# Mixing steps of DVE moved ahead of and behind the one-hots, with new shares of the one-hots and new slots for the tiles on PE

## What is computed

```python
xn = layernorm(x)
shifted = pad(xn)[:, :-1]                       # the token before
xk = xn * mix_k + shifted * (1 - mix_k)         # likewise xv and xr
k, v, r = xk @ Wk.T, xv @ Wv.T, sigmoid(xr @ Wr.T)
s = (r * wkv_scan(decay, first, k, v)) @ Wo.T
probs = softmax(xn @ w_router.T)
top_w, top_e = top_k(probs, 4); top_w /= sum(top_w)
for e in range(16):
    coeff = sum(where(top_e == e, top_w, 0))
    ffn += coeff * ((silu(xn @ w_gate[e]) * (xn @ w_up[e])) @ w_down[e])
out = x + s * silu(ffn)
```

## Time and profile before

| | us |
|---|---|
| median of 3 runs | 324.53 (323.92 to 325.04) |
| the profiled execution | 324.29 |
| its span in the trace | 322.5 |
| outside the span | 1.79 |
| PE busy | 287.6 (89% of the span) |
| DVE busy | 251.2 (78%) |
| POOL busy | 203.7 (63%) |
| ACT busy | 146.0 (45%) |

### The profile page before, as it was taken

One profiled execution on the slowest core, in us unless ns is written; L12 is line 12 of the kernel. 1 busy time (PEld: TensorE's weight loads), 2 busy tenths in 40 slices (PEclk: granted clock), 3 DMA queues, 4 the chain that ended last, 5 costly groups with the idle time before them and its releaser, 6 DMA issues.

```text
span 322.5 us, 4601 instructions
## 1 busy us (share of the span) xinstructions
PE 287.6 (89%) x1298; PEld 212.3 (66%) x1299; DVE 251.2 (78%) x523; ACT 146.0 (45%) x219; POOL 203.7 (63%) x201
## 2 busy tenths in 40 slices
PE   0698969979889999999999999999999999969960
PEld 0443424434335665888888888888888888848850
DVE  2889799986986888689299896898869961439993
ACT  1791726423267752841935536465273232312140
POOL 3600089993773767778778787787777776242281
PEclk9999979999999999999999999999999999988995
DMA  7896000016377676459655454655556578899798
GB/s 230 285 374 287 0 1 1 0 34 244 99 236 273 226 272 218 146 212 291 217 199 170 149 213 148 227 160 192 171 168 207 155 221 301 265 337 303 223 230 163
DMA packets 30379, 63.28 MB, mean 196 GB/s; under 512 B 4332, under 2 KB 20205, under 8 KB 30192
## 3 DMA queue, kind: packets, MB, share of 16 engines
q10 hardware_dynamic: 7568, 23.88, 21.2%
q0 software_dynamic: 8544, 19.41, 21.2%
q1 hardware_dynamic: 14240, 19.66, 18.1%
HBM read 50.35 MB, written 15.20 MB: 203 GB/s over the span
## 4 chain that ended last, share of the span: by engine, by line
PE 60%; DVE 16%; DMA 12%; issue 4%; ACT 3%; POOL 3%; ACTq 1%; SPq 0%; DVEq 0%; POOLq 0%
PE ps L589 52%; DMA rows<-wgu_in 5%; PE ps L696 4%; DVE arena L848 3%; DVE ohB L1007 2%; DMA y_rows<-arena,dst_idx 2%; PE ps L599 2%; DVE ohA L1002 2%; DMA wrou<-wrouT_in 1%; DMA rows<-y_rows 1%; DVE arena L1136 1%; DMA y_rows<-arena,late 1%; POOL arena L393 1%; POOL y_rows L400 1%; DVE arena L1103 1%
## 5 line engine op out<-in xcount | busy, mean ns | idle before, releaser
L589 PE MATMUL ps<-arena,rows 128*128 128x256 f32 x448 | 102.8, 384 | 3.1 <-DMA rows<-wgu_in 3.1
L393 POOL DMA_INDIRECT arena<-xn_rows,tok_idx x72 | 79.6, 1106 | 26.2 <-issue 21.6
L589 PEld LDWEIGHTS ps<-arena,rows 128*128 128x128 f32 x448 | 84.1, 193 | 13.9 <-issue 3.5
L400 POOL DMA_INDIRECT y_rows<-arena,dst_idx x60 | 65.2, 1086 | 26.2 <-issue 16.5
L589 PE MATMUL ps<-wdn,arena 128*128 x288 | 67.8, 380 | 0.4 <-DVE arena L1036 0.4
L589 PEld LDWEIGHTS ps<-wdn,arena 128*128 128x128 f32 x288 | 54.2, 191 | 7.7 <-issue 0.8
L589 PE MATMUL ps<-arena 128*128 128x512 f32 x96 | 47.1, 624 | 3.1 <-DVE arena L848 3.1
L549 ACT COPY arena<-ps 128x512 f32<-128x512 f32 x34 | 19.9, 586 | 63.9 <-PE ps L589 55.0
L375 POOL TENSOR_SCALAR ohB<-late 128x128 f16<-128x128 f32 x20 | 31.4, 1581 | 26.3 <-DVE late L924 26.3
L1036 DVE TENSOR_TENSOR arena<-arena,ps 128x512 f32<-128x512 f32 x28 | 19.1, 683 | 33.5 <-PE ps L589 15.3
L539 ACT ACTIVATE arena<-ps 128x512 f32<-128x512 f32 x36 | 21.5, 598 | 35.0 <-PE ps L589 34.9
(11 more groups left out here) (185 smaller groups left out, 370.9 us busy)
## 6 DMA issues: line engine op xcount, KB each, us to landing
rows<-wgu_in ACTq DMA_DIRECT2D x44, 512.0 KB, 3.9
rows<-y_rows SPq DMA_DIRECT2D x6, 768.0 KB, 7.2
wdn<-wd_in SPq DMA_DIRECT2D x1, 4096.0 KB, 14.9
rT<-x_in SPq DMA_DIRECT2D x4, 512.0 KB, 6.4
xn_rows<-rT SPq DMA_DIRECT2D x4, 512.0 KB, 3.3
rows<-y_rows SPq DMA_DIRECT2D x8, 256.0 KB, 4.9
out<-x_in SPq DMA_DIRECT2D x1, 1536.0 KB, 9.5
rows<-y_rows SPq DMA_DIRECT2D x3, 512.0 KB, 5.7
```

Of the source, the lines that this page charges most:

```text
L393: pool.indirect_dma_start(out=xg[i % XG][:, j, :], out_offset=None, in_=xn_rows, in_offset=bass.IndirectOffsetOnAxis(ap=tok_idx[:, 2 * i + ...
L400: pool.indirect_dma_start(out=y_rows, in_=ysb[:, par, j, :], in_offset=None, out_offset=bass.IndirectOffsetOnAxis(ap=idx[:, n + j:n + j + ...
L589: ins = nc.tensor.matmul(dst, lhsT(c), rhs(c), start=(c == 0), stop=(c == C - 1))
```

## The change

The first mixing step of the loop, (1, 0), now stands ahead of DVE's wait for the counts. The others inside the loop move up, (3, 0) stays before the one-hots of tile 11, and (3, 1) now stands behind all one-hots and ahead of DVE's wait for the last tile. DVE makes three ohB of every tile and POOL one, so 48 and 16 instead of 44 and 20. On PE a first tile is placed already after the first product of `project(1)`, and the last tiles after the first product of `project(3)`.

```diff
-        dve_slots = lambda t: 3 if t % 4 else 2
+        dve_slots = lambda t: TOPK - 1
...
             project(0, between0)
-            project(1, lambda n: place_rows((0, 1, 1, 1, 1, 2)[n]))
+            project(1, lambda n: place_rows((1, 1, 1, 1, 1, 1)[n]))
             count_ended()
-            project(2, lambda n: place_rows((1, 1, 1, 2, 1, 1)[n]))
-            project(3, lambda n: place_rows((2, 1, 0, 0, 0, 0)[n]))
+            project(2, lambda n: place_rows((1, 1, 1, 2, 1, 2)[n]))
+            project(3, lambda n: place_rows((2, 0, 0, 0, 0, 0)[n]))
...
+            mixed(1, 0)
             dve.wait_ge(count_ready, 1)
...
-            MIX_AT = {0: (1, 0), 2: (1, 1), 4: (1, 2), 6: (2, 0), 8: (2, 1), 9: (2, 2), 11: (3, 0), 13: (3, 1)}
+            MIX_AT = {0: (1, 1), 2: (1, 2), 4: (2, 0), 6: (2, 1), 8: (2, 2), 11: (3, 0)}
...
+            mixed(3, 1)
             dve.wait_ge(oh_used, T)
```

## The result

The changed kernel took 322.14 us (median of 4 runs, 320.91 to 323.57), the kernel before 324.78 on the same chip (323.92 to 328.34). The ratio is 0.9899, with a 95% interval from 0.9858 to 0.994: faster, by between 0.6% and 1.4%. The profiled execution took 323.57, with a span of 321.8; that is 0.7 less than the 324.29 and 322.5 of before, and the upper end of the four. A second measurement of the unchanged file, on another chip, gave 319.42 (6 runs, 319.16 to 323.59) against 326.4, ratio 0.9835 [0.9774 to 0.9897].

A forecast was written before the change was run, and what follows sets the result against it. PE was taken as the bound, its third-stage start mattering: projections to 78.8, indices 72.4 plus gather lag 6.31 and 0.4, so 79.1 instead of 83.03. That 3.9 us gain gave 320.4, or 320.6 as median; range 319.4 to 322.3.

The forecast's parts named there:

- The counts and the start of the loop: DVE before the one-hots: mixing step (1, 0) makes the counts 0.35 to 0.4 us later, one-hots starting at 41.98.
- The idle time of PE: PE ahead of tile 0: idles 3.25 us until 45.0, replacing the old wait, with product 6 already done.
- DVE's loop: DVE's one-hot loop: shrinks from about 29.9 to 27.6 us, ending at 69.6.
- The near tie: Last two tiles, second stage: PE gets there at 69.0 us, DVE's last one-hot comes at 69.6.
- PE has only 0.6 us in hand: PE after tile 0's wait: 0.6 us of slack; a half-clock stretch would lose 1.67 and make PE late by 1.1.
- the likeliest case: Whole kernel: gain 3.9 us as summed, half clock off the path, time 320.6 us; chance 0.55.
- The second rival: PE's second stage: half clock on the path in most executions, gain only 3.0 us, time 321.5; chance 0.22.
- (3, 1) and the indices: DVE behind the one-hots: (3, 1) runs 69.6 to 70.95, delaying the indices about 1 us, to 72.4.
- The gather: Indices to third stage: lag 6.31 us plus 0.4 for sharing DMA with weight loads; without the 0.4, 78.7 beside PE's 78.8.
- a meeting without any rub: Start of third stage: PE, DVE and POOL meet smoothly and the gather is free, giving 78.4 and 4.6 us gain.
- The fourth rival: Third stage near 286 us: the last-weights wait grows by the gain, its load meeting reads of y; 324.3 to 324.6; chance 0.05.
- The fifth rival: One-hot loop: POOL stands still under DVE's one-hots too, adding 12.7 us to the loop, about 332.8 us; chance 0.05.

The follow-up runs named there:

- after_again: The changed kernel without an edit, measured again on another chip: median 319.42 us of 6 runs, ratio 0.9835 to the kernel before.
- fill_fit: Changed kernel plus thrown-away PE matmuls in two waits, 14 ahead of tile 0 and 7 ahead of the last batch's routing: 321.56 us, ratio 0.9874.
- undo_slots: Changed kernel with the tiles placed on PE in their old slots: median 319.37 us of 4 runs, ratio 0.9896 to the kernel before.
- undo_slots2: Changed kernel with the tiles in their old slots on PE, measured a second time: median 321.29 us of 6 runs, ratio 0.9878.
- after: The changed kernel as first measured and profiled: median 322.14 us of 4 runs, ratio 0.9899; the profiled execution took 323.57.
- probe: Changed kernel with scratch work added ahead of the one-hot loop, 18 POOL one-hots beside four kinds of DVE instruction: 347.31 us, no comparison.
- undo_shares: Changed kernel with the old one-hot shares, 44 on DVE and 20 on POOL: median 322.8 us of 10 runs, ratio 0.9939.
- best: Changed kernel with the x-to-out copy later, mixing steps moved behind tile 0, two POOL one-hots at tiles 7 and 12: 323.24 us, ratio 0.9849.

## Why the prediction was right, and where not

**The counts and the start of the loop.** Predicted 0.35 to 0.4 later, at 41.98. In after_again they came 0.43 and 0.44 later (35.18, 42.04): right. In the first profile the loop began at 44.29, from a slow product at 15 us and a half-clock stretch at 31.2, neither of them in the sum.

**The idle time of PE.** Predicted 3.25 us, a wait of the same length in place of the old one, with one product more behind it; measured 3.17, and 3.49 in after_again. Right.

**DVE's loop.** Predicted 27.6; 27.63 in two profiles. The number was right for partly wrong reasons: the loop holds waits for PE of 0.50 us (0.23 + 0.27), and without the half clock it takes 27.15 (fill_fit).

**PE's placing, and the tie.** Predicted 24.0 us from tile 0 to the last two; 24.10 in fill_fit, with PE there 27.35 us behind the loop's start and DVE ready at 27.15. The near tie was real.

**"PE has only 0.6 us in hand".** This is the step that failed. I took DVE as the later of the two by 0.6 us, and let the likeliest case leave the half clock off the path. All five profiles with the new slots, the mixing table of the change or nearly so, and no filling have the stretch behind the idle time, PE had nothing in hand, and the whole 1.68 us reached the first L696 (fill_fit). The second rival, which I gave 0.22, is what the stage did: it put the first L696 at 80.0, and after_again has it at 80.05. What neither case saw is that the gathers stand behind it as the next limit: without the half clock PE starts sooner, waits 1.15 to 1.54 us for rows, and is level again (undo_slots, undo_slots2). That the stretch cost nothing in the kernel before is not shown either: behind it DVE waited 0.59 us for PE, before 50.50, the idle time that the sum takes out of the loop.

The Trainium skill says in TensorE: Matmul & The Clock Gate (Part 1: The HAM clock gate) that the moment at which the clock changes varies from run to run. The trace agrees for the counts, where a stretch from about 31 us on came in two of fourteen profiles (after, and at 31.4 the probe, ahead of its added work); at tile 0, behind 3.1 to 3.5 us of idling, it came every time, in five profiles.

**POOL.** Predicted 25.6 us behind the loop's start and the waits at tiles 10 and 12 gone. It was 27.05, 1.4 later (it waits for buffers that PE frees, six times 0.26 to 0.50), and the two waits are gone. The shares were not needed for that: undo_shares has no such waits either.

**(3, 1) and the indices.** Predicted 30.4 behind the loop's start, measured 31.03. That (3, 1) would delay the indices by 1 us did not happen: DVE was done with it 0.60 us before the tile was, since the tile came with PE.

**The gather.** The lag was to be 6.31 + 0.4 and a tie with PE. From the end of the indices (75.32) to the first L696 it was 6.98 here, but PE took the rows without waiting, directly behind the last product, so this is no longer the gather's lag. In undo_slots, where PE waited 0.28 for them, it was 36.54 - 30.82 = 5.72: the extra 0.4 was not there, nor even the whole 6.31. What I missed is the unit behind: I costed the first gather alone, while the following ones hang on the same indices.

**The end.** Predicted 79.1 for the start of the third stage, 3.9 us gained. Measured 80.05 in after_again, 3.0, and 0.73 in the first profile. Against the loop's start the gain is 3.42; without the half clock it would have been 5.10 (41.43 - 36.33), which is 78.4 with a loop that starts at 42.04, the value that I gave for a meeting without any rub.

**The third stage.** I let each microsecond reach the end. In after_again the span is 4.9 us shorter, not 3.0, but the lead changes on its way. By the fifth group it is 4.8: the waits of 0.48 for gathered rows and 0.75 for weights are gone, worth 1.9 us. Where the scatter meets the copy 0.25 is lost. Then comes the wait for the last weights; before, and in after_again:

```profile
289.11 5.12 PE L589 MATMUL ps<-arena,rows 128*128 128x256 f32 x16 [3.12 <-DMA rows<-wgu_in]
...
283.72 3.72 PE L589 MATMUL ps<-arena,rows 128*128 128x256 f32 x16 [2.30 <-issue]
```

The idle time is 0.8 shorter, and no stretch at half clock follows it, which gives another 1.4: the last products start 6.8 us sooner (290.73 against 297.53). Of these 1.9 are lost behind them, where DVE's last sums wait for the rows of y to be read back (2.2 us in all, 0.3 before). So the 4.9 are a sum of gains and losses that my forecast had none of, and that they come near the 4.8 of the fifth group is chance. In the first profile the same 1.9 were won, and 1.4 given back at 159 us; its wait for the last weights (2.52 us before 287.27) had its half clock, and from there on another 0.9 was lost.

The fourth rival, gain given back, was right in kind: something is given back, but not at the last weights, where both profiles win. It is lost where the scatter meets the copy and at the end, where y is read back. At the copy PE waits between 0 and 1.8 us, depending on the profile, and I did not find what decides it.

**The fifth rival**, POOL standing still under DVE's one-hots, is refuted by the probe (0.85 to 0.96).

**The number.** 320.6 lies between the two medians of the changed kernel, 322.14 and 319.42, and both lie in the range from 319.4 to 322.3. That it fits so well is in part luck: it has 0.9 us too much gain for the stage (79.1 against 80.05), and waits in the third stage, won and lost, are not in the sum. The two profiled executions are 4.2 us apart: 2.2 of it comes ahead of the stage, 1.2 at the copy, 1.8 by the wait and the clock at the last weights, and 1.0 goes the other way at the end. So executions of one kernel differ by more than the 0.3% that I had counted with. How much of the difference between the medians comes from such chances, and how much from the chip, stays open.

## What to carry to other kernels

Undo a change part by part in the profile, count from the last event that all versions share, and compare at two depths: at the first transposes one moved line had brought 3.31 of 3.42 us and the new slots had cost 1.5, and at the fifth group the line was worth 3.2 of 5.35 and the slots nothing, because PE then waited for the gathered rows. When a change makes an idle time of TensorE, look at the clock in the stretch behind it and ask whether the engine has anything in hand there, and then what it would wait for next. And what DVE does beside POOL matters by its kind: take the fp32 steps out from under POOL's work before giving its work away.

## What the runs showed of the hardware

In the second stage an idle time of PE of 3.1 to 3.5 us was followed by a stretch at 1.2 GHz of 3.4 us in all six profiles that had one; the seven with 0 to 2.16 us ahead of tile 0 had none. The length of the idle time alone does not tell the two apart: elsewhere 2.06 us (fill_fit, before 92.63) and 2.19 (best, before 233.42) were followed by such a stretch, and 2.30 (after_again, before 283.72) was not. One stretch cost 1.68 us where PE was the pace.

A stretch of the same kind also fell while PE was busy with small matmuls (31.2 to 34.6, and at 31.4 in the probe's profile), about 1 us behind an idle time of 1.59. The kernel before idled 1.60 in the same place, and its clock stayed up. No row shows what set it off.

One POOL one-hot took 0.79 us alone and 4.90 beside twelve fp32 `tensor_scalar` of DVE with one SBUF input. I had expected that of two-input instructions only, and a one-hot beside `tensor_tensor` took 1.45 to 2.35, against 4.30 under two mixing steps and one ohA in the kernel.

A scatter of rows took 8.36 us beside a 1.5 MB copy. Moving the copy by 81 us moved the wait by 73 (from 159 to 233 us).
